# Cross-attention over 32 batches: the Gram product in 32-column tiles, y transposed a step ahead

## What is computed

```python
# layer 0, twice (x queries y, and y queries x), per batch and head
attn = softmax(einsum('ni,nj->ij', q, k) * 16**-0.5)      # q = x' Wq', k = y' Wk'
out  = (v @ attn) @ proj.T                                # v = y' Wv'
x1   = x + res_p2r + y + res_r2p
# layer 1: q, k = Wq y + bq, Wk y + bk; v = Wv x1 + bv
scores = einsum('hdl,hel->hde', q, k) / sqrt(128)
o      = Wo @ (softmax(scores) @ v) + bo + x1
result = (o - mean(o)) * rsqrt(var(o) + 1e-5) * gn_w + gn_b   # over the whole batch entry
```

## Time and profile before

| | |
|---|---|
| median of 3 runs | 336.73 us (336.71 to 337.72) |
| the profiled execution | 336.78 us |
| its span | 335.0 us |
| PE busy | 322.2 us (96%), 2566 matmul records |
| PEld, DVE, ACT, POOL busy | 268.6, 261.4, 234.8, 188.3 us |
| chain that ended last | PE 92% of the span, DVE 3%, issue 2% |
| Gram (L372) in that chain | 34% of the span |
| DMA | 73.73 MB, mean 220 GB/s |

### The profile page before, as it was taken

How to read it: one execution, slowest core, us unless ns; L and a number is a source line. 1 busy time by engine, 2 the same in 40 slices (tenths; PEclk the granted TensorE clock), 3 DMA queues, 4 the chain that set the end, 5 groups by cost and what they waited for, 6 DMA issues and landing times.

```text
span 335.0 us, 8099 instructions
## 1 busy us (share of the span) xinstructions
PE 322.2 (96%) x2566; PEld 268.6 (80%) x2566; DVE 261.4 (78%) x677; ACT 234.8 (70%) x382; POOL 188.3 (56%) x277
## 2 busy tenths in 40 slices
PE   7999999999999999999999999999999999999980
PEld 5788888897888889797888879788888978887750
DVE  2565997979698797969789796969979796983774
ACT  3646868778686877778677787867787786865332
POOL 0973892855829194673909476491928558291010
PEclk9999999999999999999999999999999999999995
DMA  7996899799696969979697978969597990203014
GB/s 233 391 287 180 239 284 280 207 305 258 204 297 175 313 161 294 247 241 286 170 302 196 274 222 270 294 168 314 168 299 178 296 268 14 112 0 127 1 58 193
DMA packets 39050, 73.73 MB, mean 220 GB/s; under 512 B 4608, under 2 KB 26368, under 8 KB 39040
## 3 DMA queue, kind: packets, MB, share of 16 engines
q1 hardware_dynamic: 35008, 58.92, 62.5%
q10 hardware_dynamic: 4032, 14.68, 12.1%
HBM read 56.81 MB, written 16.78 MB: 220 GB/s over the span
## 4 chain that ended last, share of the span: by engine, by line
PE 92%; DVE 3%; issue 2%; DMA 1%; ACT 1%; SPq 0%; POOLq 0%; POOL 0%
PE gacc L372 34%; PE oacc L392 10%; PE oacc L393 9%; PE oacc L397 9%; PE mid L482 4%; PE mid L416 4%; PE mid L459 4%; PE tpx L329 4%; PE mid L468 3%; PE mid L419 2%; PE mid L469 2%; PE mid L429 1%; DMA raw<-in_ctx 1%; PE mid L471 1%; PE mid L470 1%
## 5 line engine op out<-in xcount | busy, mean ns | idle before, releaser
L1034 POOL TENSOR_TENSOR xy_lo<-raw,xy_hi 128x256 fp32r<-128x256 f32 x256 | 177.8, 736 | 116.2 <-ACT xy_hi L642 116.2
L372 PE MATMUL gacc<-t 128*128 128x257 f32 x512 | 124.7, 385 | 0.8 <-ACT t L574 0.8
L372 PEld LDWEIGHTS gacc<-t 128*128 128x128 f32 x512 | 93.2, 190 | 15.6 <-issue 2.6
L642 ACT ACTIVATE xy_hi<-raw 128x1024 fp32r<-128x1024 f32 x64 | 67.1, 1051 | 0.0
L792 DVE STREAM_TRANSPOSE t<-y_blocks 128x512 f32<-128x512 f32 x56 | 63.9, 1141 | 0.0
L392 PE MATMUL oacc<-xy_hi,pq_hi 128*128 128x512 f32 x124 | 51.9, 418 | 0.3 <-ACT pq_hi L621 0.2
L393 PE MATMUL oacc<-xy_lo,pq_hi 128*128 128x512 f32 x124 | 49.0, 395 | 0.0
L649 ACT ACTIVATE res<-oacc 128x512 f32<-128x512 f32 x60 | 35.7, 596 | 11.4 <-PE oacc L397 9.6
L813 DVE BATCH_NORM_STATS2 hstat<-res 128x6 f32<-128x512 f32 x60 | 39.4, 677 | 1.4 <-ACT res L649 1.4
L397 PE MATMUL oacc<-xy_hi,pq_lo 128*128 128x512 f32 x124 | 38.9, 394 | 0.0
L663 ACT ACTIVATE res<-res,nbias,nscale 128x1024 f32<-128x1024 f32 x29 | 35.9, 1237 | 0.5
(11 more groups left out here) (117 smaller groups left out, 456.3 us busy)
## 6 DMA issues: line engine op xcount, KB each, us to landing
raw<-in_x SPq DMA_DIRECT2D x31, 512.0 KB, 4.4
raw<-in_ctx SPq DMA_DIRECT2D x31, 512.0 KB, 6.1
y_blocks<-in_ctx SPq DMA_DIRECT2D x112, 128.0 KB, 5.1
out<-res ACTq DMA_DIRECT2D x28, 512.0 KB, 3.5
x_blocks<-in_x SPq DMA_DIRECT2D x56, 128.0 KB, 4.9
out<-res SPq DMA_DIRECT2D x4, 512.0 KB, 2.6
wt<-in_weights SPq DMA_DIRECT2D x1, 896.0 KB, 6.8
raw<-in_x SPq DMA_DIRECT2D x2, 256.0 KB, 3.4
```

The costliest lines, as they stand in the source:

```text
L372: mm = pe.matmul(gacc[:, 0:2 * C + 1], t[slot][:, c, C:2 * C], t[slot][:, c, :], start=(c == 0), stop=(c == CH - 1))
L642: act.activation(xy_hi[slot][:, s, :], raw[slot][:, s, :], ACT.Copy).then_inc(split_hi, 1)
L1034: piece = pool.tensor_tensor(xy_lo[slot][:, s, cols], raw[slot][:, s, cols], xy_hi[slot][:, s, cols].bitcast(f32), ALU.subtract)
```

## The change

Gram: t's row becomes y' (0 to 127), ones (128), x' (129 to 256): XC = 129, GW = 257. Each chunk's product is done by six matmuls, each with 32 columns of y' as the stationary side and a 32-partition piece of the bank as its output (four column tiles of the array). Of Y Y' four 32 x 32 blocks, that are mirrors of others, are left out, so each tile gets 225 of 257 columns. The batches of a pair now use a bank each (gacc, and columns 64 to 320 of stat). A new function of DVE, gram_mirror, fills the four blocks in gram by transposing their mirrors.

PE's order: Gram of both batches stands in one piece behind the scores, with z_products behind its last chunk but one; the out_halves of batch 1 follow z, m_products end the step, and pq_products of a pair move to the next step, ahead of u12_products. u_products is split in u12_products and u3_products, which waits for gram_mirror and pq_low. group_moments, the variance, norm_scale, normalise and store of a pair come a step later than before.

DVE: y of batch 0 is transposed a step ahead. The attention is written by one multiply over 128 x 6 x 2 x 32, with sinv2, the reciprocal sums times a 0/1 mask (own_half), in place of four. ACT and POOL follow the new order. SP's loads are split in refill_raw and refill_blocks, and the first steps load more blocks in advance. PE, ACT and POOL have two more steps written out and six turns of the loop, DVE four more and five turns; SP keeps its six.

```diff
+XC = C + 1
+GW = XC + C
+        sinv2 = sb("sinv2", [C, 6, 2])
+        own_half = sb("own_half", [C, 2])
-        mean_s, abv_s = stat[:, 16:18], stat[:, 32:34]
+        mean_s, abv_s = stat[:, 16:18], mid0[:, 12 * W32:12 * W32 + 2]
+        gacc_b = [gacc[:, 0:GW], stat[:, H64:H64 + GW]]
...
                 for c in range(begin, end):
-                    mm = pe.matmul(gacc[:, 0:2 * C + 1], t[slot][:, c, C:2 * C], t[slot][:, c, :],
-                                   start=(c == 0), stop=(c == CH - 1))
+                    first, final = c == 0, c == CH - 1
+                    wa, wb, wc, wd = (tb[:, c, W32 * j:W32 * (j + 1)] for j in range(QUADS))
+                    pe.matmul(acc[0:W32, C:GW], wa, tb[:, c, C:GW], start=first, stop=False)
+                    pe.matmul(acc[3 * W32:C, 3 * W32:GW], wd, tb[:, c, 3 * W32:GW], start=first, stop=False)
+                    pe.matmul(acc[W32:H64, W32:GW], wb, tb[:, c, W32:GW], start=first, stop=final)
+                    pe.matmul(acc[H64:3 * W32, W32:GW], wc, tb[:, c, W32:GW], start=first, stop=final)
+                    pe.matmul(acc[0:W32, 0:3 * W32], wa, tb[:, c, 0:3 * W32], start=False, stop=final)
+                    mm = pe.matmul(acc[3 * W32:C, 0:H64], wd, tb[:, c, 0:H64], start=False, stop=final)
...
+            def u3_products(p):
+
+                pe.wait_ge(gram_full, p + 1)
+                if not (isinstance(p, int) and p < 1):
+                    pe.wait_ge(pqlo_ready, p)
...
                 elif front:
                     x_transpose(h, u, 0)
                     x_transpose(h, u, 1)
-                    u_products(p - 1)
+                    pq_products(p - 2)
+                    u12_products(p - 1)
                     out_half(h - 1, u, 0, 0)
+                    u3_products(p - 1)
+                    if post:
+                        group_moments(p - 3)
                     out_half(h - 1, u, 0, 1)
                     scores(p - 1)
+                    gram_chunks(h, u, 0, 0, 4)
+                    gram_chunks(h, u, 0, 4, 8)
+                    if post:
+                        pe.wait_ge(var_ready, p - 2)
+                    gram_chunks(h, u, 1, 0, 4)
+                    gram_chunks(h, u, 1, 4, 7)
+                    z_operands(p - 1)
+                    gram_chunks(h, u, 1, 7, 8)
+                    z_products(p - 1)
                     out_half(h - 1, u, 1, 0)
                     out_half(h - 1, u, 1, 1)
-                    gram_chunks(h, u, 0, 0, 3)
-                    z_operands(p - 1)
-                    gram_chunks(h, u, 0, 3, 4)
-                    z_products(p - 1)
-                    gram_chunks(h, u, 0, 4, 8)
-                    group_moments(p - 2)
                     m_products(p - 1, False)
-                    gram_chunks(h, u, 1, 0, 4)
-                    pq_products(p - 1)
-                    gram_chunks(h, u, 1, 4, 8)
...
+                elif front:
+                    split_high(*(h - 1 + u, 1 - u), 1, 1, post)
+                    xt_out(h, u, 0, 0)
+                    pq_high(p - 2, u)
+                    u12_out(p - 1)
+                    xt_out(h, u, 0, 1)
+                    keys_times_sums(p - 1)
+                    out_to_sbuf(h - 1, u, 0, 0)
+                    out_to_sbuf(h - 1, u, 0, 1)
+                    if post:
+                        norm_scale(p - 3)
+                        normalise(*before(h, u), 0)
+                    exponent(p - 1)
...
+            def gram_mirror(p):
+
+                dve.wait_ge(gram_ready, 2 * p + 2)
+                for i, j in ((0, 3), (1, 0), (2, 0), (3, 2)):
+                    rows, cols = slice(W32 * i, W32 * (i + 1)), slice(W32 * j, W32 * (j + 1))
+                    last = dve.transpose(gram[rows, :, cols], gram[cols, :, rows])
+                last.then_inc(gram_full, 1)
...
+                dve.tensor_tensor(attn[:, :, :].rearrange("p i (s c) -> p i s c", c=W32),
+                                  probs.unsqueeze(2).broadcast_to([C, 6, 2, W32]),
+                                  sinv2[:, :, :].unsqueeze(3).broadcast_to([C, 6, 2, W32]), ALU.mult).then_inc(attn_ready, 1)
...
                 elif front:
-                    y_transpose(h, u, 0, 0)
+                    if post:
+                        half_stats(*before(h, u), 1, 1)
+                        half_moments(p - 3)
+                        partition_moments(p - 3, 1 - u)
+                    y_transpose(h, u, 1, 0)
+                    pq_low(p - 2, u)
+                    y_transpose(h, u, 1, 1)
+                    u3_out(p - 1)
+                    if post:
+                        variance(p - 3, 1 - u)
                     x_transpose(h, u, 0)
-                    u3_out(p - 1)
-                    y_transpose(h, u, 0, 1)
+                    shift_scores(p - 1)
                     x_transpose(h, u, 1)
+                    softmax_out(p - 1)
                     half_stats(h - 1, u, 0, 0)
-                    shift_scores(p - 1)
                     half_stats(h - 1, u, 0, 1)
-                    softmax_out(p - 1)
+                    if ahead:
+                        y_transpose(h + u, 1 - u, 0, 0)
+                        y_transpose(h + u, 1 - u, 0, 1)
+                    gram_mirror(p)
                     half_stats(h - 1, u, 1, 0)
                     n12_out(p - 1)
                     n3_out(p - 1)
                     c_out(p - 1, 1 - u)
```

More of the change, by code:

```diff
@@ L195, in steps, with before @@
         def steps(eng, step):
[L196 to L202, removed]
+            step(0, 0, True, False, False, False)
+            step(0, 1, True, True, False, False)
+            step(1, 0, True, True, True, False)
+            step(1, 1, True, True, True, True)
+            with eng.Fori(2, PAIRS // 2) as i:
+                step(i, 0, True, True, True, True)
+                step(i, 1, True, True, True, True)
+            step(PAIRS // 2, 0, False, True, True, True)
+            step(PAIRS // 2, 1, False, False, True, True)
+        def before(h, u):
+            return (h - 1, 0) if u == 1 else (h - 2, 1)
         BOTH = slice(0, 2)
@@ L280, in store, with step @@
                 sp.dma_start(out[q], res[2 * u + b][:, :]).then_inc(stored[2 * u + b], 16)
[L282 to L291, removed]
+            def step(h, u):
+                refill_blocks(h, u, 0)
+                refill_raw(h - 1 + u, 1 - u, 1)
+                refill_blocks(h, u, 1)
+                refill_raw(h, u, 0)
+            refill_raw(0, 0, 0)
+            refill_raw(0, 0, 1)
+            refill_raw(0, 1, 0)
             with sp.Fori(1, PAIRS // 2 - 1) as i:
-                step(i, 0, True, True, True)
-                step(i, 1, True, True, True)
+                step(i, 0)
+                step(i, 1)
             last = PAIRS // 2 - 1
[L296 to L299, removed]
+            refill_raw(last - 1, 1, 1)
+            store(last + 1, 0, 0, True)
+            store(last + 1, 0, 1, True)
+            store(last + 1, 1, 0, False)
+            store(last + 1, 1, 1, False)
             for n in range(4):
@@ L484, in pq_products, with step @@
                 mm.then_inc(pq_done, 1)
-            def step(h, u, front, middle, back):
+            def step(h, u, front, middle, back, post):
                 p = 2 * h + u
@@ L584, in keys_times_sums @@
                 for a in range(2):
[L585 removed]
+                    last = act.activation(sk[:, a, :], w("kT"), ACT.Copy, scale=gram[:, a, C:XC])
                 last.then_inc(sk_ready, 1)
@@ L946, in c_out, with step @@
                     .then_inc(c_ready, 1)
-            def step(h, u, front, middle, back):
+            def step(h, u, front, middle, back, post, ahead=True):
                 p = 2 * h + u
@@ L985, in step @@
                     c_out(p - 1, 1 - u)
-                    y_transpose(h, u, 1, 1)
-                    pq_low(p - 1, 1 - u)
                 elif middle:
+                    half_stats(*before(h, u), 1, 1)
+                    half_moments(p - 3)
+                    partition_moments(p - 3, 1 - u)
+                    pq_low(p - 2, u)
+                    variance(p - 3, 1 - u)
                     u3_out(p - 1)
@@ L1018, in step @@
                     normalise_last(h - 1, u, 1, 1)
-            steps(dve, step)
+            last = PAIRS // 2 - 1
+            step(0, 0, True, False, False, False)
+            step(0, 1, True, True, False, False)
+            step(1, 0, True, True, True, False)
+            step(1, 1, True, True, True, True)
+            with dve.Fori(2, last) as i:
+                step(i, 0, True, True, True, True)
+                step(i, 1, True, True, True, True)
+            step(last, 0, True, True, True, True)
+            step(last, 1, True, True, True, True, ahead=False)
+            step(last + 1, 0, False, True, True, True)
+            step(last + 1, 1, False, False, True, True)
         @block.gpsimd
@@ L1048, in step @@
                     split_low(h, u, 1, 0)
```

(9 more changed lines are left out.)

216 lines of the change are left out of this document (111 added, 105 removed).

## The result

The changed kernel takes 345.14 us (median); the kernel before, run beside it, 337.23. The ratio is 1.022 (95% interval 1.019 to 1.024). An execution more than 1.5% above the fastest of its kernel counts as slow and is left out of every ratio, here one of 350.12 us. The forecast was 331.5 in a range of 323 to 341, faster. It is slower, and outside the range. The profiled execution took 345.86 us with a span of 344.1, so the span is 9.1 longer than before.

The account below looks back on a forecast made before the run. PE's queue was taken as the bound. A step of 18.18 + 0.65 = 18.83 us saves 6.2 us over 14 steps; with head -1.4 and tail +2.3, span 335.0 becomes 329.7, time 331.5 us, range 323 to 341.

Parts of the forecast that it names:

- The head: Stretch up to the first full step: 34.02 becomes 32.6 us, from cheaper Gram chunks and the moved pq_products.
- Rival D: Slower: PE's doubled loop body no longer stays in, each of five returns waits for instruction fetch; +10, 341.5 us; chance 0.12.
- Gram in tiles: PE's Gram: four column tiles run side by side, 0.388 us a chunk instead of 0.435; 1.05 us less a step.
- F: Rival: the Gram's tiles don't overlap, in strict program order; 0.785 us a chunk, 433 us; chance 0.02.
- C: Rival, slower or the same: a tile's weights arrive too late in the Gram, 8.2 us more, 339.7 us; chance 0.20.
- PE's own work: PE's queue in one loop step without waits: 19.27 - 1.05 - 0.24 + 0.20 = 18.18 us.
- The wait at L397: Third quarter of the first out_half waits for DVE's pq_low: 0.65 us a step, bounds 0.3 and 1.2.
- the sign that I had set: The prediction counts as wrong if a loop step is under 18.3 or over 19.2 us.
- Tail: From the last loop step to the first out of the last pair: 14.9 us grows by 2.3, bounds 1.2 and 3.5.
- DVE and the rest: Attention multiply -0.67 us, mirror +0.8 us a step; DVE stays at about 16.2 of 18.8 us; y ahead costs nothing.
- rival E: Slower: DVE takes the bound, with mirror and attention multiply at their upper bounds; about 337 us; chance 0.07.
- The likeliest case: The forecast itself: 331.5 us, own range 328 to 334; chance 0.45.

Follow-up runs that it names:

- pq_lo kernel: Changed kernel with VectorE's subtraction that makes pq_lo moved ahead of the first y transpose of the step: 342.20 us, ratio 1.017 to the kernel before.
- later block loads: Changed kernel with the 12 block loads of the fourth pair moved behind the first two pairs' raw refills on SyncE's queue: 345.98 us, ratio 1.025.
- ScalarE's tail: Changed kernel with out-half evictions and exponent ahead of the scale and two normalisations in ScalarE's first step behind the loop: 343.14 us, ratio 1.015.
- four steps in a turn: Changed kernel with four steps instead of two in a turn of TensorE's loop, same instructions in the same order: 367.14 us in one execution.
- light loads: Kernel with four steps per TensorE loop turn, every load inside SyncE's loop cut to a quarter of its columns or blocks: 346.61 us in one execution.

## Why the prediction was wrong

**The head, -1.4 against +7.7: the step that failed.** Of the 14.4 us between forecast and measured span, 9.1 lie here, 3.8 in the steps and 1.7 in the tail (the rest gives 0.2 back). Rival D had the cause, instruction fetch, at the wrong place. It asked only whether the loop's body stays in, and it does: q8 is silent from 117 us, near the end of the first turn, to 315 us. Its own row, four packets between 20 and 70 us, showed that all fetching happens in the straight-line head and the loop's first turn, and I put its cost at nothing there because PE's queue had covered it. But that cover is made of time for each instruction: before, two steps of 38.5 us had 664 instructions, 14.8 us for a block of 256, and in the full-array Gram it was 28 us (four instructions in 0.435 us). In the tiled Gram it is 4.1. I had counted the matmuls (317 a step) and never divided time by them. Taking the tiles out of the head gave back 6.0 us there, from 41.76 to 35.76; the 1.7 us that remain over 34.02 end in an ordinary wait for x.

The Trainium skill (Runtime: NRT & Kernel Launch, Instruction fetch mechanics) was cited for a room of 2048 instructions. The runs agree with it as far as they go: 1311 stay in, 2622 don't.

**Gram in tiles: right.** 0.381 us a chunk against 0.388, and z at 0.82 against 0.81. The lower bound was added up wrongly: 450 columns at 0.81 ns are 0.365 and not 0.375. In the timeline of one chunk four tiles start together:

```profile
164.65 0.29 PE L390 MATMUL gacc<-t 128*32 128x129 f32 x1
164.66 0.32 PE L391 MATMUL gacc<-t 128*32 128x161 f32 x1
164.67 0.38 PE L392 MATMUL gacc<-t 128*32 128x225 f32 x1
164.67 0.38 PE L393 MATMUL gacc<-t 128*32 128x225 f32 x1
164.78 0.27 PE L390 MATMUL gacc<-t 128*32 128x129 f32 x1
```

A's second pass (L390) starts 0.11 us after the other tiles have begun. That it stands ahead of theirs in the program shows at the first late block, where A's first pass ran alone at 25.73 us and its second and all of D, B and C only at 28.43. This contradicts the rule of strict order in the Trainium skill (TensorE: Matmul & The Clock Gate, Part 3), and with it rivals F and C are out.

**PE's own work, 18.18 a step: 0.3 too low.** The pq_lo kernel has it almost bare, 18.76, of which 0.27 is the wait for pq_high: 18.49. The pieces that came out larger than in my sum: the out_halves 5.96 with z's return in them, against 5.60 + 0.20 (an out_half behind other products begins with a pass 0.10 longer, and there are now three such places a step), the transposes 0.07, the Gram 0.08, the scores 0.05. The m products came out 0.08 smaller.

**The wait at L397 (now L419): there, smaller, and at L419 only in every second step of the loop.** 0.65 was forecast for each step. (PE's side of it, 1.53 + 0.89 + 0.89 + 0.87 + 0.93, is 5.1 and not 5.2.) Measured are 0.41 at L419 in the first step of VectorE's five turns, 0.10 in each at u3 (L446 follows L419 by 0.56, in the pq_lo kernel by 0.46), which wants pq_lo too, and 0.27 in each for pq_high, which was only in my upper bound. On the mean of such a pair that is 0.58, near the forecast by size, and 18.49 + 0.58 is 19.07, where two steps of the loop measure 38.17. Over all 14 steps the mean is 19.10, with the 1.57 us of the third late block in it. By the sign that I had set, a step over 19.2 us, four of the five slow steps (19.27 to 19.29) and the first one (20.08) show the sum of the step wrong. That one edit removed the 0.41 and the 0.10 shows that the queue position of pq_low was its cause.

**Tail, +2.3 against +4.0.** The sum had 0.89 for pq_products, 0.6 for pq_lo and 0.8 because the exponent stands behind two normalises. pq_lo costs 0.52, at u3. The third term had the right queue and the wrong wait. The exponent (319.03 us) stands behind one normalise, ended by then, and waits for VectorE's L960; z shows no wait. What is late is ScalarE's evictions: the first (316.64) stands behind norm_scale, which waits until 315.74 for GpSimd's rstd, the second (319.26) behind the exponent. The two out_halves that need their banks wait 0.95 and 1.30 us from start to start against 0.24, 1.77 in place of 0.8. Another 0.59, PE's wait for nmat ahead of pq_products, had no term at all.

**DVE and the rest: right, and without effect.** Four mirror transposes take 0.99 us (0.8), the multiply 0.56 (0.56), attn comes well ahead of z; rival E didn't occur (its sum takes 0.9 for the mirror where its own bounds give 0.8). y a step ahead caused no wait that the profile shows.

**The chances.** The likeliest case was given 0.45 although its head was a difference of guesses. D's price of five times 2 us at the returns came near the truth (341.5 against 345) by the wrong route, which is luck; the changed kernel has no wait at a return.

## What to carry to other kernels

Before a matmul is cut into several small ones, divide the time of the stretch by its instructions: where 256 of them last about 4 us and stand in straight-line code beside full DMA queues, a block can cost up to 4 us (0.2 to 4.1 here, and some cost nothing); at 15 us and more none did. Keep such code in a loop whose body stays in (here 1311 instructions; its first turn is still loaded), and the written-out steps in few, long instructions. After a reordering look at each eviction or subtraction that someone waits for, and at what stands ahead of it on its engine: one line moved on VectorE gave 3.2 us over 14 steps.

## What the hardware showed that I had not expected

- TensorE's instructions came in packets of 16 KB over a DMA queue of their own, and PE went on 1.4 us after a late one had landed. With a DMA share of 0.79 reloading cost 23.6 us in nine steps, with 0.32 it cost 3.4.
- Which block is late depends on its place and on chance: one position near 25.7 us cost 2.4, 3.3 and 4.1 us in three kernels (the changed one, later block loads, ScalarE's tail) with the same TensorE program, and nothing when the program was 128 instructions longer.
- The clock added to the price. From 36.9 to 40.3 us, behind 3.87 us without work, it was granted at 0.50 (1.2 GHz), and a chunk of the Gram took 0.75 us instead of 0.381. In the kernel with four steps in a turn PE's own work over nine steps was 7.4 us longer than with light loads.
- At five steps, the starts of VectorE's own five turns, VectorE needs 3.02 to 3.18 us from the start of c_out to that of pq_lo, elsewhere in the full steps 2.75 to 2.77, with the same nine counted operations between them. Where VectorE's steps are written out and PE's still loop, it is 2.76. The views leave register instructions out; the records have at least five of them between the two at these five places (seven at four of them), and at most two elsewhere. So they are the likely reason; no run changed them.
